# 16-head attention: queries turned by a pair of transposing DMAs per batch, keys turned in two parts, a third score bank

## The reference

```
Q = split_heads(query, NUM_HEADS) * dh ** (-0.5)      # 16 heads of 16, or 8 heads of 32
Kh, Vh = split_heads(k_mem, NUM_HEADS), split_heads(v_mem, NUM_HEADS)
logits = einsum('bhqd,bhkd->bhqk', Q, Kh) + b
logits = logits + MASK_VALUE * (1.0 - valid)[:, None, None, :]
weights = softmax(logits, axis=-1)
out = einsum('bhqk,bhkd->bhqd', weights, Vh)
```

## Time and profile before

| | |
|---|---|
| median of 3 runs | 3040.35 us (3040.26 to 3041.69) |
| profiled execution | 3040.6 us, span 3038.8 us |
| TensorE (PE) busy | 2477.8 us, 82% |
| VectorE (DVE) busy | 2118.2 us, 70% |
| ScalarE (ACT) busy | 1277.5 us, 42% |
| GpSimd (POOL) busy | 1032.8 us, 34% |
| mean granted TensorE clock | 0.912 |
| scores of l0a | first 65.6, last 289.1 us |
| scores of l2a | first 1531.9, last 1691.5 us |
| scores of l2s | first 1820.4, last 2026.4 us |
| scores of l3a | first 2720.4, last 2881.1 us |

### The profile page before, as it was taken

How to read it: one execution, slowest core, us unless ns; L and a number is a source line. 1 busy time by engine, 2 the same in 40 slices (tenths; PEclk the granted TensorE clock), 3 DMA queues, 4 the chain that set the end, 5 groups by cost and what they waited for, 6 DMA issues and landing times. The chain is left out here.

```text
span 3038.8 us, 56011 instructions
## 1 busy us (share of the span) xinstructions
PE 2477.8 (82%) x20572; PEld 1607.4 (53%) x20572; DVE 2118.2 (70%) x5472; ACT 1277.5 (42%) x2264; POOL 1032.8 (34%) x1445
## 2 busy tenths in 40 slices
PE   1999286999915589997989778985999999969973
PEld 0444264666614358995556544444565555646662
DVE  5998764766577666665677688977765545866668
ACT  1788452323222223332367646771322222257722
POOL 3452272110074361114467397851300000025330
PEclk9999598999957699998989888997999999979996
DMA  3331274443150347775653131100100000024301
GB/s 99 126 126 72 77 259 142 105 111 104 36 159 11 100 170 269 260 257 177 202 121 94 32 126 41 45 12 10 60 22 1 1 1 1 1 58 100 73 10 61
DMA packets 252738, 283.35 MB, mean 93 GB/s; under 512 B 125659, under 2 KB 200713, under 8 KB 246452
## 3 DMA queue, kind: packets, MB, share of 16 engines
q1 hardware_dynamic: 225780, 203.50, 22.1%
q0 software_dynamic: 17904, 76.23, 7.3%
q10 hardware_dynamic: 8784, 0.04, 0.2%
HBM read 166.60 MB, written 88.34 MB: 84 GB/s over the span
## 5 line engine op out<-in xcount | busy, mean ns | idle before, releaser
L1647 ACT ACTIVATE l2e_hf<-l2e_H 128x512 f32<-128x512 f32 x208 | 124.2, 597 | 381.8 <-PE l2e_H L1590 381.8
L1779 POOL TENSOR_TENSOR all_m_rstd<-all_m_sq,all_mhalf 128x8 f32<-128x8 f32 x24 | 39.6, 1649 | 559.9 <-DVE all_m_sq L1764 525.6
L1590 PE MATMUL l0e_H<-l0e_xT,l0e_w 128*128 128x512 f16 x768 | 168.9, 382 | 27.1 <-DVE l0e_w L1662 27.1
L1686 DVE CAST l2e_hh<-l2e_hf 128x512 f16<-128x512 f32 x208 | 92.7, 446 | 122.9 <-ACT l2e_hf L1647 108.7
L825 DVE TENSOR_REDUCE l0a_mx<-l0a_S 128x2 f16<-128x512 f32 x256 | 166.5, 683 | 12.5 <-PE l0a_S L650 10.5
L1590 PE MATMUL l2e_H<-l2o_hi,l2e_w 128*128 128x512 f16 x576 | 151.8, 382 | 15.8 <-DVE l2e_w L1662 15.8
L821 DVE CUSTOM_DVE_ANT_0 l2s_masked<-l2s_S,l2s_mq 128x128 f32<-128x128 f32 (+1 forms) x512 | 152.9, 349 | 16.0 <-PE l2s_S L650 11.7
L1647 ACT ACTIVATE l0e_hf<-l0e_H 128x512 f32<-128x512 f32 x128 | 76.4, 597 | 206.4 <-PE l0e_H L1590 206.4
L774 ACT ACTIVATE l0a_pf<-l0a_ST 128x512 f32<-128x512 f32 x256 | 146.2, 600 | 38.5 <-PE l0a_ST L664 37.5
L1590 PE MATMUL l1e_H<-l1e_xT,l1e_w 128*128 128x256 f16 (+1 forms) x1404 | 158.3, 274 | 4.1 <-DMA l1e_w<-packed,all_second_weight_row 4.1
L1590 PE MATMUL l2e_H<-l2e_hh,l2e_w 128*128 128x512 f16 x640 | 155.2, 379 | 0.0
(11 more groups left out here) (696 smaller groups left out, 7065.4 us busy)
## 6 DMA issues: line engine op xcount, KB each, us to landing
l0e_wf<-in_L_ffn_w SPq DMA_DIRECT2D x16, 1024.0 KB, 7.4
rows<-l0a_zeros SPq DMA_DIRECT2D x16, 640.0 KB, 6.1
l1e_rb<-rows SPq DMA_DIRECT2D x39, 256.0 KB, 8.1
results<-l1e_y SPq DMA_DIRECT2D x39, 256.0 KB, 2.2
l0a_kv<-in_ctx SPq DMA_DIRECT2D x16, 512.0 KB, 4.3
rows<-l0a_zeros SPq DMA_DIRECT2D x16, 512.0 KB, 5.1
l0d_p_cx<-in_ctx SPq DMA_DIRECT2D x16, 512.0 KB, 6.7
results<-l0e_y SPq DMA_DIRECT2D x16, 512.0 KB, 3.2
```

What stands on the lines that cost most here:

```text
L1590: mm = pe.matmul(bank[0:fn, :], W[par][0:kn, at + k * wd + f0:at + k * wd + f0 + fn], X, start=(done == 0), stop=(done == k_all - 1))
L1647: nc.scalar.activation(hf[q % 4][0:fn, :], pair_of(q, lay)[0][0:fn, :], lay.func, scale=1.0 / WS).then_inc(acted, 1)
L1686: nc.vector.tensor_copy(high, v).then_inc(hi_done, 1)
L1779: self.nc.gpsimd.tensor_tensor(out=(self.rstd, self.rstd2)[which][:, g], in0=(self.sq, self.sq2)[which][:, g], in1=self.g.mhalf[:, 0:self. ...
```

## The change

In the 16-head stages the queries are no longer turned by TensorE and copied by VectorE. SyncE turns them by one pair of transposing DMAs of 128x1024 per batch, issued at slot 4 of even halves; `qT` becomes three buffers of a whole batch (also with 8 heads, where the pairs stay 128x512, one per half). The keys of a half are turned in two parts of four transposes, at slots 5 and 7, in the first four places of one PSUM bank `K_ps`; ScalarE copies the parts at slot 6 and at slot 1 of the next half. The turned maxima take the last two places of the same bank in the 16-head stages, and a bank of their own with 8 heads. The freed bank is a third bank for scores with 16 heads: score n waits for the maxima of head n - 3.

```diff
-    BACK_AT, MAX_AT, TURN_Q_AT, TURN_K_AT = (1, 2, 5, 7) if heads == 16 else (1, 1, 3, 3)
-    COPY_AT, DIV_AT, KEYS_AT, SUM_AT = (3, 2, 1, 5) if heads == 16 else (2, 3, 1, 3)
+    wide = heads == 16
+    SB = 3 if wide else 2
+    BACK_AT, MAX_AT, TURN_Q_AT, TURN_K_AT = (1, 2, 4, (5, 7)) if wide else (1, 1, 3, (3,))
+    COPY_AT, DIV_AT, KEYS_AT, SUM_AT = (3, 2, ((2, 6), (1, 1)), 5) if wide else (2, 3, ((1, 1),), 3)
+    PARTS = len(TURN_K_AT)
+    QP = 1 if wide else 2
+    CP = 4 // PARTS
...
-        qT = [st.sb(f"qT{i}", [P, 4, S], F16) for i in range(RING)]
+        qT = [st.sb(f"qT{i}", [P, 8, S], F16) for i in range(RING // 2)]
...
-        S_ps = [st.ps(f"S{i}") for i in range(2)]
+        S_ps = [st.ps(f"S{i}") for i in range(SB)]
-        MH_ps = [st.ps(f"M{i}", [P, 8, P], F16) for i in range(2)]
-        N_ps = MH_ps[0]
+        K_ps = st.ps("K", [P, 6 if wide else 8, P], F16)
+        N_ps = K_ps[0:HALF, 4:6, :] if wide else st.ps("N", [HALF, TB, P], F16)[:, :, :]
...
+                def turn_queries(b, a):
+                    if a == 0:
+                        sp.wait_ge(stacked, b + 1)
...
+                    elif a == 0:
+                        sp.wait_ge(q_in[b % 2], b // 2 * 32 * QP)
+                    else:
+                        sp.wait_ge(q_in[b % 2], b // 2 * 32 * QP + 32)
+                    if a == 0 and b >= RING // 2:
+                        sp.wait_ge(scoredT, (b - RING // 2 + 1) * heads)
                     v = qs[b % 2][:, :, :, :].rearrange("p t h r -> p t (h r)")
+                    c = slice(a * 8 // QP, (a + 1) * 8 // QP)
                     for u in range(TB):
+                        sp.dma_start_transpose(qT[b % (RING // 2)][:, c, u * P:u * P + P],
+                                               v[:, u, c.start * P:c.stop * P]).then_inc(q_in[b % 2], 16)
...
-                    if by_dma and i == TURN_Q_AT and 0 <= j + 2 < NH:
-                        turn_queries(j + 2)
+                    if i == TURN_Q_AT and 0 <= j + 2 < NH and j % 2 < QP:
+                        turn_queries((j + 2) // 2, j % 2)
...
-                            pool.wait_ge(chunks, per_batch * (b - 1))
-                            for a in range(2 if by_dma else 0):
-                                pool.wait_ge(q_in[a], (b - 1) * 16 * TB)
+                            pool.wait_ge(chunks, 2 * PARTS * (b - 1))
+                            pool.wait_ge(q_in[b % 2], b // 2 * 32 * QP)
...
-                        if n >= 2:
-                            pe.wait_ge(maxed, n - 1)
+                            b = h // 2
+                            pe.wait_ge(q_in[b % 2], b // 2 * 32 * QP + 32 * min(h % 2 + 1, QP))
+                            pe.wait_ge(k_turned, (h + 1) * PARTS)
+                        if n >= SB:
+                            pe.wait_ge(maxed, n - SB + 1)
...
+                def turn_keys(h, part):
                     b = h // 2
                     pe.wait_ge(stacked, b + 1)
...
+                    if h or part:
+                        pe.wait_ge(k_turned, h * PARTS + part)
+                    if wide and h >= 3:
                         pe.wait_ge(nm_rows, h - 2)
+                    v = ks[b % 2][:, :, :, :].rearrange("p t h r -> p t (h r)")
+                    for c in range(CP):
+                        for u in range(TB):
+                            j = h % 2 * 4 + part * CP + c
+                            m = pe.transpose(K_ps[:, c * TB + u, :], v[:, u, j * P:j * P + P], ident_h[:, :])
+                    m.then_inc(chunks, 1)
 
                 def turn_max(h):
                     pe.wait_ge(maxed, (h + 1) * HALF)
-                    if not by_dma:
-                        pe.wait_ge(q_turned, min(h + 3, NH))
-                    elif h:
+                    if h:
                         pe.wait_ge(nm_rows, h)
+                    if wide:
+                        pe.wait_ge(k_turned, min(h + 3, NH) * PARTS)
...
+                def copy_keys(h, part):
+                    act.wait_ge(chunks, h * PARTS + part + 1)
+                    if h >= RING and part == 0:
                         act.wait_ge(scoredT, (h - RING + 1) * HALF)
+                    nc.scalar.activation(kT[h % RING][:, part * CP:(part + 1) * CP, :],
+                                         K_ps[:, 0:CP * TB, :].rearrange("p (c u) q -> p c (u q)", c=CP), ACT.Copy
                                          ).then_inc(k_turned, 1)
...
-                def copy_queries(h):
-                    dve.wait_ge(chunks, 2 * h + 1)
-                    if h >= RING:
-                        dve.wait_ge(scoredT, (h - RING + 1) * HALF)
-                    nc.vector.tensor_copy(qT[h % RING][:, :, :],
-                                          MH_ps[0][:, :, :].rearrange("p (c u) q -> p c (u q)", c=4)
-                                          ).then_inc(q_turned, 1)
...
-                    if not by_dma and i == 0 and 0 <= j + 1 < NH:
-                        copy_queries(j + 1)
```

More of the change, by code:

```diff
@@ L466, in attention_stage @@
         k_hi, v_set, stacked = st.sem("k_hi"), st.sem("v_set"), st.sem("stacked")
-        chunks, q_turned, k_turned = st.sem("chunks"), st.sem("q_turned"), st.sem("k_turned")
+        chunks, k_turned = st.sem("chunks"), st.sem("k_turned")
         q_in = [st.sem(f"q_in{i}") for i in range(2)]
@@ L533, in _ @@
                             row = a * rows + aux + 2
-                            sp.dma_start(qT[h % RING][row:row + 1, 0:HALF // per, :], nmT[h % 2][a:HALF:per, :]
-                                         ).then_inc(nm_in[h % 2], 16)
-                    if by_dma and i == TURN_Q_AT and 0 <= j + 2 < NH:
-                        turn_queries(j + 2)
+                            c0 = h % 2 * 4
+                            sp.dma_start(qT[h // 2 % (RING // 2)][row:row + 1, c0:c0 + HALF // per, :],
+                                         nmT[h % 2][a:HALF:per, :]).then_inc(nm_in[h % 2], 16)
+                    if i == TURN_Q_AT and 0 <= j + 2 < NH and j % 2 < QP:
+                        turn_queries((j + 2) // 2, j % 2)
                 for i in range(len(clears)):
@@ L642, in score @@
                         if n % HALF == 0:
[L643 to L647, removed]
-                        if n >= 2:
-                            pe.wait_ge(maxed, n - 1)
-                    m = pe.matmul(S_ps[n % 2][:, s_at[u]:s_at[u] + key_to[u]],
-                                  qT[h % RING][r0:r0 + rows, j, u * P:u * P + P],
+                            b = h // 2
[3 more added lines that the diff above has]
+                            pe.wait_ge(maxed, n - SB + 1)
+                    m = pe.matmul(S_ps[n % SB][:, s_at[u]:s_at[u] + key_to[u]],
+                                  qT[h // 2 % (RING // 2)][r0:r0 + rows, h % 2 * 4 + j, u * P:u * P + P],
                                   kT[h % RING][r0:r0 + rows, j, 0:key_to[u]], start=True, stop=True)
@@ L665, in scoreT @@
                                   kT[h % RING][r0:r0 + rows, j, u * P:u * P + P],
-                                  qT[h % RING][r0:r0 + rows, j, query_from[u]:S], start=True, stop=True)
+                                  qT[h // 2 % (RING // 2)][r0:r0 + rows, h % 2 * 4 + j, query_from[u]:S], start=True, stop=True)
                     if u == TB - 1:
@@ L717, in turn_max @@
+                    m.then_inc(chunks, 1)
                 def turn_max(h):
                     pe.wait_ge(maxed, (h + 1) * HALF)
-                    if not by_dma:
-                        pe.wait_ge(q_turned, min(h + 3, NH))
-                    elif h:
+                    if h:
                         pe.wait_ge(nm_rows, h)
+                    if wide:
+                        pe.wait_ge(k_turned, min(h + 3, NH) * PARTS)
                     for u in range(TB):
-                        m = pe.transpose(N_ps[0:HALF, u, :], mx[h % 2][:, u, :], ident_h[:, :])
+                        m = pe.transpose(N_ps[:, u, :], mx[h % 2][:, u, :], ident_h[:, :])
@@ L748, in _ @@
                         turn_max(j - 1)
[L749 to L752, removed]
+                    if i in TURN_K_AT and 0 <= j + 2 < NH:
+                        turn_keys(j + 2, TURN_K_AT.index(i))
             @block.scalar
             def _(act):
-                def copy_keys(h):
-                    act.wait_ge(chunks, h + 1 if by_dma else 2 * h + 2)
-                    if by_dma and h >= RING:
+                def copy_keys(h, part):
+                    act.wait_ge(chunks, h * PARTS + part + 1)
+                    if h >= RING and part == 0:
                         act.wait_ge(scoredT, (h - RING + 1) * HALF)
-                    nc.scalar.activation(kT[h % RING][:, :, :],
-                                         MH_ps[1][:, :, :].rearrange("p (c u) q -> p c (u q)", c=4), ACT.Copy
+                    nc.scalar.activation(kT[h % RING][:, part * CP:(part + 1) * CP, :],
+                                         K_ps[:, 0:CP * TB, :].rearrange("p (c u) q -> p c (u q)", c=CP), ACT.Copy
```

(7 more changed lines are left out.)

24 lines of the change are left out of this document (4 added, 20 removed).

## The result

The changed kernel takes 3005.12 us, median of 4 runs (3001.96 to 3007.06), against 3041.02 (3040.26 to 3042.69, 4 runs) of the kernel before on the same chip: ratio 0.988, 95% interval 0.9868 to 0.9892. The forecast of 3010 lay 5 us too high. The profiled execution took 3007.06 us, its span is 3005.3 us.

The account below looks back on a forecast made before the run. TensorE and VectorE were taken to bound l0a in a loop, with GpSimd close in l2s. Gains of 21.4 in l0a and 11.5 in l2s, less 2 for the starts, made -31 us from 3040.6: forecast 3010, range 3000 to 3020.

Parts of the forecast that it names:

- Bound and loop in l0a: l0a: TensorE and VectorE hold each other; slot 5's scores wait for maxima(3), 0.49 a half, gone with the third bank.
- The ScalarE stall of 0.25: l0a, slots 7 and 0: new waits for ScalarE's copy and exponential add 0.25, making 6.35 a half.
- TensorE's part: l0a: queries' turn goes (-0.66), cutting the keys' turn adds a switch (+0.21); TensorE needs 6.10 a half.
- would be 0.49 again: l0a, slot 5: without the third bank the wait for maxima(3) would remain, 0.49 a half.
- GpSimd's stall: l2s, odd half, slot 6: the weighing waits for GpSimd's cuts, 1.1, making that half 6.36.
- 0.56 of waits: l2s, even half: 0.22 late behind GpSimd plus 0.34 from two ScalarE waits, making that half 5.82.
- The transposing pair: Sync queue, 16-head stages: the queries' pair lands in 6.9, hidden by 0.5 to 0.9 in rooms of 7.75 and 7.4.
- X: Time of the transposing pair from issue to landing, taken as 6.9 us.
- Rival B: Transposes land late, slot 0 of even halves waits; 16 us per us late in each stage; chance 0.08 mild, 0.18 beyond.
- some 190 us each: Slowdown of both 16-head stages if sixteen 128x128 blocks a batch were turned one after another, 20.9 us; the prediction doubted it.
- Counting 31 halves: Both 16-head stages: a saving per half counts 31 times, 32 halves with one shared with the filling.
- the starts: First scores of l0a and l2s come later because of the first transposes; +2 us for both together.

Follow-up runs that it names:

- the DMAs alone: Changed kernel with two score banks, keys turned in one part at slot 7 and copied at slot 1, maxima in their own bank: 3031.65 us, ratio 0.9957.

## Why the prediction was right, point by point

- **Bound and loop in l0a: shown.** The bank wait at slot 5 was 0.49 and is gone; with two banks it is back and the run is 14 us longer (against the trace of the changed kernel run again, l0a by 12.3 and l2s by 6.0, where 7.5 and 2 had been expected). The half is 6.34 to 6.35, forecast 6.35; the batch 12.69, forecast 12.70; (14.07 - 12.69) x 15.5 = 21.4, as forecast.
- **The ScalarE stall of 0.25: shown.** In the trace it is 0.10 at the second half turn and 0.12 at slot 0 (its score at 157.17, its turned score at 157.29). Copying the sums two slots later took 0.20 of it away, to 6.15 a half. The copy of 512 elements took 0.59 to 0.63, forecast 0.60.
- **"A turn costs 0.66" (TensorE's part): right only beside the third bank.** By itself, with two banks, it gave 0.28 (turn of queries off slot 5: 7.04 to 6.76) or 0.37 (to 6.67) of 0.66. The note in the prediction that the stall "would be 0.49 again" without the bank is near for the change as it is, with the keys in two parts: a half is 6.67 there, 6.10 + 0.49 + 0.08. It does not hold for the DMAs alone, where a second wait stands at slot 6 or 0.
- **l2s: the mechanism shown, the sum right partly by luck.** The batch was 12.11 to 12.13, forecast 12.18; (12.92 - 12.12) x 15.5 = 12.4 gained, forecast 11.5. But from slot 0 to the next slot 0 the odd half took 6.64 and the even one 5.47, forecast 6.36 and 5.82: two errors that cancel. In the odd half GpSimd's stall was 1.21, forecast 1.10, and the weighing started 5.47 after slot 0 (1865.18 to 1870.65), forecast 5.19. In the even half 0.56 of waits were added to 5.26, and 0.21 came. (The 5.26 stands in the prediction without its working; with the 0.21 of switching that it took for l0a it is 5.31, and the gain 9.9.) Moving the stacking took the stall away.
- **The transposing pair: hidden, but the term was mis-sized.** I doubled the issue with the width (5.02); it stayed 2.61. X was 4.5, not 6.9, so the room of 7.5 (slot 0 at 150.82, pair at 156.05, batch of 12.69) is left with 3, not 0.9. Rival B, to which I gave 0.26, was therefore much less likely than that, and the first scores came at 64.6, not 66.0. Its price was too low as well: 16 us per us late leaves the clock out (108.6 us of waits went with 148 us). The figure cited from the Trainium skill (VectorE: DVE Perf Modes, "The three transpose paths"), 1309 ns for a DMA transpose of 128x128, does not hold as a price per block in this trace either: 1.32 us issues eight such blocks, and sixteen had landed after 4.5. The estimate of "some 190 us each" worked out from it is too low by the prediction's own price: 16 x (20.9 - 7.75) and 16 x (20.9 - 7.4) are 210 and 216.
- **Counting 31 halves: too few.** The stages gained 24.1 and 16.3 where full halves account for 21.4 and 12.4. The 6.6 left fall into the first four halves and the last ones, where the copy and the turns also went; I had no term for it. With the starts (-1.0 and +0.6 where +2 was taken, 2.4) and 0.9 more in l2s's batches this is 9.9 beyond the forecast; the 8-head stages (5.4) and the stretches between the stages (1.9) took 7.3 of it back. 31 + 9.9 - 7.3 is the 33.5 of the table, to 0.1. That the total came within 5 us is thus partly luck: two terms that were left out nearly cancel.
- **The 8-head stages: "nothing" was 5.4.** l2a is 4.5 longer and l3a 0.9. In l2a most of it is the start: the first 28 us after the first score have a granted clock of 0.50 (8.1 us), then 0.88 (20 us), where the kernel before had 0.68 and 1.00 in the same stretches:

```profile
1506.60:1514.70 8.10, 7.22 (x38) 3.91 (x39) 5.37 (x10) 1.89 (x2) 4.72 (x9) 0.50 0.51 130
1514.70:1534.70 20.00, 17.52 (x136) 10.23 (x134) 10.93 (x20) 12.98 (x20) 12.48 (x21) 0.88 0.50 107
```

  All ten traces with the new code of l2a have 162.2 to 164.9 us in l2a and a clock of 0.50 in the first 8.1 us, the one trace of before 159.6. In the middle of the stage a half takes 5.18 in all eleven, so the difference is mostly in the first four halves. The three new traces with 0.96 or 0.97 in the second stretch have 162.2 to 162.5, the seven with 0.88 or 0.89 have 163.9 to 164.9. Whether the bank of the maxima or the changed order on the queue brings it about was not tried; it stays open.

## What to carry to other kernels

Work taken off a bounding engine is a gain in full only if it did not cover another engine's wait: lay out where the next wait falls, and move the buffer count with it (here the DMA alone gained 12 us, the third bank and the split keys 24 more). Count a buffer's last reader as well as its first: one pair of transposing DMAs early in a batch frees the stack in time, two pairs, half of them late, cost more than everything gained. When a stall is taken away, the next is usually one of order, not of totals; two edits of the order alone gave another 21 us.

## What the runs showed of the hardware that had not been expected

- A transposing DMA costs its queue about the same at 128x512 (1.26 us) and at 128x1024 (1.32 us); from issue to landing it takes 2.5 (l2s) to 2.8 us (l0a) and 3.2 (l0a) to 3.6 us (l2s), all medians. Wide ones are half the price per element on the queue.
- After 3.5 us without scores TensorE's granted clock was 0.50 in the next 3.1 us window and 0.68 in the one behind it. The waits of 3.4 us on average, 16 in each of two stages, sum to 108.6 us, and the run was 148 us longer.
